# Two attentions and eight experts on one core: four batches' inputs at the head of the queue, the first unit's transposed scores moved ahead, row maxima in one transfer

## The chip, the cores and the metric

The kernel runs on one core of one Trainium2 chip. A core has five engines that run side by side, each with its own instruction stream, in order: PE (matrix multiply, which reads SBUF and writes PSUM), DVE (vector), ACT (scalar functions), POOL (general vector work) and SP (here it only issues transfers). Sixteen DMA engines serve the core; the transfers of this case are put on them mostly by SP, some by ACT and POOL. Engines meet through semaphores: an instruction may wait until a semaphore has reached a value, and raise another one when it is done.

The metric is the device time in microseconds of one execution. The kernel before took 696.34 us, the median of 3 runs (694.67 to 696.98).

## The reference

Eight batches of 256 tokens with 256 features, all in float32. The three stages follow one another:

```
x = layernorm(x + attn(x))      # 16 heads of 16, causal window of 64 keys, Wqkv, bqkv, Wo, bo
x = layernorm(x + xattn(x, ctx))# q = relu(x Wq + bq), k, v = relu(ctx W + b), causal over 256 keys,
                                # softmax(q k / 4) v + q, layer norm with gamma and beta
x = layernorm(x + ffn(x))       # 8 experts, top 2 of a softmax router, capacity 160 per expert
                                # in each of 2 groups of 1024 tokens, relu(x wi) wo, 256 -> 1024 -> 256
```

## The kernel before

**Units.** One attention of one batch is a unit; there are 16, in the order of the list UNITS: self-attention ("s") of batches 0 to 3, then cross-attention ("c") and self-attention in turn. The units 0 to 3 are all self-attention. Everything below is about the first four units, that is the first 100 us.

**What a unit does.** PE projects q and k (QS, KS; line 485; 8 matmuls each, into one of three PSUM banks "work"). ACT adds the bias and rounds to bf16 (line 717), DVE makes two more bf16 parts of what was rounded off (SQ and SK; lines 873, 877, 878), so that three bf16 parts stand for one float32. SP then copies the parts into a tile "arena", six copies for q and six for k, so that a head's six products of parts lie below one another in 96 partitions (line 413). With that, PE makes scores twice:

- The natural scores (jobs N 0 to 11, lines 537 for the mask and 541 for the products, bank "nat"): queries in the partitions. DVE takes the negated maximum of each row (line 926). When all 12 are done, DVE splits the maxima in three bf16 parts (MP, 934 to 937), PE transposes them (MT, 571), ACT copies them to the tile mT (48 rows of 256; line 761), and a transfer writes them as three more rows, partitions 96 to 98, below q's stack (line 425).
- The transposed scores (jobs T 0 to 11, same lines, bank "byk"): keys in the partitions, 99 partitions deep. k's stack has ones in the last three rows, so the maxima are subtracted in the product. ACT takes exp (775) into probs, and after each three jobs PE multiplies with v (PV 0 to 3, line 606), ACT copies the result out (784).

V's projection is VS (line 492), and DVE adds its bias (906). The three rows of ones below each k stack are filled once, for all four stacks, by four transfers at line 364; T 0 of unit 0 waits for them and for the maxima's rows (lines 578 to 580).

**What sets the order.** A function in_order gives every step a slot, a number, and sorts. All engines walk the same list, each doing its part of a step; so the slots set the order on every engine and on SP's queue of transfers. One unit begins every 12 slots (n0). A unit's N jobs stand at n0 to n0 + 11 and its T jobs at n0 + 18 to n0 + 29, so T 0 to T 5 of a unit interleave with N 6 to N 11 of the next, and T 6 to T 11 with N 0 to N 5 of the one after that. QS stands at n0 - 19, KS at n0 - 17.5. LOADS (line 57) gives slots to 13 loads (LD, line 354): V's weights and bias at -10 and -9.9, the rows of ones at -9.8, x of batch 2 at -4, x of batch 3 at 8. SP does them in turn with its other steps, and an SP step that waits holds up all that stand behind it.

Of the kernel before, what the change touches and what calls it, by code (L numbers as in the profile page):

```python
# [6 lines left out]
BF16 = mybir.dt.bfloat16  # L7
# [5 lines left out]
P = 128  # L13
# [11 lines left out]
MR = 3  # L25
# [31 lines left out]
LOADS = (-10, -9.9, -9.8, -4, 8, 15, 15.1, 19, 19.1, 28, 32, 40, 50)  # L57
# [11 lines left out]
def in_order():  # L69
# [6 lines left out]
    for k, (layer, b) in enumerate(UNITS):  # L76
        n0 = first_slot(k)
        if layer == "s":
            for later, earlier in X_BEFORE.items():
                if earlier == b:  # L80
                    add(n0 + 9.6, "LX", UNIT_OF["s", later])
# [77 lines left out]
def attention_and_experts(nc: bass.Bass, a, out):  # L159
    with ExitStack() as ctx:  # L160
# [75 lines left out]
        onesb = sb("onesb", [P, P], BF16)  # L236
# [46 lines left out]
        ident_ready = sem("ident_ready"); masks_ready = sem("masks_ready"); pool_consts = sem("pool_consts"); ones_in = sem("ones_in")  # L283
# [63 lines left out]
        def _(sp):  # L347
# [5 lines left out]

            def LD(i, n, layer, b):

                if i == 0:
                    sp.dma_start(ws[:, :, 2 * D:3 * D], a["w_s_v"]).then_inc(w_s_v_in, 16)
                elif i == 1:
                    sp.dma_start(rows[:, 0:1, :], a["rows"][0:1, :].partition_broadcast(P)).then_inc(bv_in, 16)
                elif i == 2:  # L360
                    sp.wait_ge(pool_cols, 1)
                    ones_rows = arena[KR:KR + MR, :].bitcast(BF16).rearrange("p (i n a b) -> p i n a b", i=PAIRS, n=2, b=P)[:, :, 1, :, :]
                    for pair in range(PAIRS):
                        sp.dma_start(ones_rows[:, pair, :, :], onesb[0:MR, :].unsqueeze(1).broadcast_to([MR, H * T // P, P]))\
                            .then_inc(ones_in, 16)
                elif i == 3:
                    sp.dma_start(x_T(2), a["x_T"][2]).then_inc(x_in[2], 16)
                elif i == 4:
                    sp.dma_start(x_T(3), a["x_T"][3]).then_inc(x_in[3], 16)
                elif i == 5:  # L370
                    sp.dma_start(rows[:, 1:5, :], a["rows"][1:5, :].partition_broadcast(P)).then_inc(rows_in, 16)
                elif i == 6:
                    sp.dma_start(woT[:, :, :], a["w_s_o"]).then_inc(w_s_o_in, 16)
                elif i == 7:
                    sp.dma_start(wc["k"][:, :, :], a["w_c_k"]).then_inc(wc_in["k"], 16)
                elif i == 8:
                    sp.dma_start(cT[:, 0, :, :], a["ctx_T"][0]).then_inc(c_in[0], 16)
                elif i == 9:
                    sp.dma_start(wc["q"][:, :, :], a["w_c_q"]).then_inc(wc_in["q"], 16)
                elif i == 10:  # L380
                    sp.dma_start(cT[:, 1, :, :], a["ctx_T"][1]).then_inc(c_in[1], 16)
                elif i == 11:
# [88 lines left out]
        def _(pe):  # L471
# [103 lines left out]
            def T_(k, j, layer, b):  # L575
                q, ks = stack["q", k % PAIRS], stack["k", k % PAIRS]
                if j == 0:
                    pe.wait_ge(m_rows[k % 2], 16 * MR * (k // 2 + 1))
# [71 lines left out]
            def GP(n, _, layer, b):  # L650
# [3 lines left out]
                def emit(bank):  # L654
                    nc.tensor.matmul(bank[:, 0:NG], tri[:, :], choice[:, n, :], start=True, stop=True)
                    return nc.tensor.matmul(bank[:, NG:2 * NG], onesb[:, :], choice[:, n, :], start=False, stop=True, skip_group_check=True)
# [51 lines left out]
        def _(act):  # L708
# [49 lines left out]
            def MT(k, n, layer, b):  # L758
                bank = computed(act, "MT", k)
                wait(act, m_rows[k % 2], 16 * MR * (k // 2))  # L760
                nc.scalar.activation(mT[:, k % 2, :], bank[0:MR * H, :].bitcast(BF16)[:, 0:T], ACT.Copy).then_inc(released("MT", k), 1)

# [88 lines left out]
        def _(dve):  # L851
# [9 lines left out]
            V.memset(eps[:, :], EPS).then_inc(eps_ready, 1)  # L861
            V.memset(mp[:, :, :, :], 0.0)
# [254 lines left out]
        def _(pool):  # L1117
# [13 lines left out]

            g_.memset(ident[:, :], 0.0)
# [23 lines left out]
            g_.memset(onesb[:, :], 1.0).then_inc(pool_cols, 1)  # L1156
            g_.memset(tri[:, :], 1.0)
# [133 lines left out]
```

## Time and profile before

| | |
|---|---|
| median of 3 runs | 696.34 us |
| the profiled execution | 695.47 us, its span 693.6 us |
| PE busy | 546.2 us, 79% of the span |
| DVE busy | 338.3 us, 49% |
| ACT busy | 218.4 us, 31% |
| POOL busy | 146.7 us, 21% |
| granted TensorE clock, mean | 0.902 |
| DMA queue of SP | 47.69 MB, 41.5% of 16 engines |

The profile page cuts the span in 40 slices of 17.3 us and gives the busy share of each in tenths. PE's row begins 5 2 3 5 9 4 9 8 7 9: of the first six slices, up to 104 us, four are half empty or worse, while later ones mostly stand at 8 or 9. The row of the DMA engines' busy share begins 4 9 5 9 7 5. Both rows are averages; which wait ends last in a stretch is read from the timeline and the list of waits.

### The profile page before, as it was taken

What the parts mean: (1) busy time and instruction counts of PE and PEld (TensorE: products, weight loads), DVE (VectorE), ACT (ScalarE), POOL (GpSimd) and SP (SyncE); (2) the same over time, 40 slices, a digit from 0 to 9 for tenths busy, and PEclk for the clock granted to TensorE, in tenths of its full rate; (3) what the DMA queues carried; (4) which work ended last, traced back from release to release, by engine and by line L of the source; (5) the groups of instructions that cost most, each with busy time, mean ns of one, the idle gap of its engine ahead of it and who ended that gap; (6) DMA issues with size and microseconds to landing.
All of it is one profiled execution on the core that took longest, in us unless ns stands there. A gap on an engine that the chain in (4) does not pass through costs nothing.

```text
span 693.6 us, 12865 instructions
## 1 busy us (share of the span) xinstructions
PE 546.2 (79%) x5092; PEld 422.1 (61%) x5092; DVE 338.3 (49%) x952; ACT 218.4 (31%) x491; POOL 146.7 (21%) x160
## 2 busy tenths in 40 slices
PE   5235949879898998997988678998787977998970
PEld 4122736656675766665766445777576866787860
DVE  4415615667577676776688547633334001222113
ACT  2000424354254453444536233353110100213103
POOL 4000002021021021030241560001111562322320
PEclk9557879999999998999999887899987999999995
DMA  4959756754945944944584553445655212688214
GB/s 97 127 63 140 131 82 110 109 97 75 140 90 88 130 81 85 115 59 69 73 109 63 93 144 79 148 170 176 213 184 168 57 39 59 173 257 288 32 13 131
DMA packets 58503, 78.96 MB, mean 114 GB/s; under 512 B 9630, under 2 KB 51997, under 8 KB 55372
## 3 DMA queue, kind: packets, MB, share of 16 engines
q1 hardware_dynamic: 48844, 47.69, 41.5%
q10 hardware_dynamic: 3456, 25.17, 9.9%
q0 software_dynamic: 6144, 5.29, 4.7%
q8 instruction: 40, 0.66, 0.4%
q14 instruction: 19, 0.16, 0.1%
HBM read 40.32 MB, written 13.74 MB: 78 GB/s over the span
## 4 chain that ended last, share of the span: by engine, by line
PE 32%; DVE 9%; issue 9%; DMA 3%; ACT 3%; SPq 1%; POOL 1%; another core or an unknown queue 0%; ACTq 0%; POOLq 0%; DVEq 0%
PE work L680 10%; PE work L694 8%; PE work L697 2%; PE work L485 2%; PE pv L606 2%; DVE negm L926 1%; PE work L665 1%; PE byk L541 1%; PE work L479 1%; PE byk L537 1%; DVE stats_c L941 1%; DVE r_c L997 1%; DMA arena<-in_ffn_wi 1%; PE work L645 1%; PE nat L541 1%
## 5 line engine op out<-in xcount | busy, mean ns | idle before, releaser
L926 DVE TENSOR_REDUCE negm<-nat 128x4 f32<-128x512 f32 (+2 forms) x192 | 120.4, 641 | 126.5 <-PE nat L541 121.5
L775 ACT ACTIVATE probs<-byk 128x512 f32<-128x512 f32 (+1 forms) x192 | 106.5, 563 | 120.2 <-PE byk L541 118.2
L541 PE MATMUL nat<-arena 96*128 96x128 bf16 (+2 forms) x512 | 74.4, 249 | 0.0
L541 PE MATMUL byk<-arena 99*128 99x128 bf16 (+2 forms) x512 | 73.3, 246 | 0.0
L541 PEld LDWEIGHTS byk<-arena 99*128 99x128 bf16 x512 | 46.6, 101 | 18.9 <-issue 2.7
L541 PEld LDWEIGHTS nat<-arena 96*128 96x128 bf16 x512 | 47.3, 102 | 17.3 <-issue 3.8
L537 PE MATMUL nat<-window_q,identb 128*128 128x384 bf16 (+1 forms) x96 | 36.2, 378 | 19.4 <-DMA arena<-parts_k 13.5
L680 PE MATMUL work<-yn_T,arena 128*128 128x160 f32 x256 | 42.3, 321 | 10.7 <-issue 5.4
L680 PE MATMUL work<-woT,arena 128*128 128x160 f32 x256 | 44.9, 333 | 4.2 <-issue 4.0
L1180 POOL TENSOR_TENSOR resk<-fk,parts_k 128x512 f32<-128x512 f32 x8 | 9.3, 1160 | 172.7 <-ACT fk L717 113.7
L680 PEld LDWEIGHTS work<-yn_T,arena 128*128 128x128 f32 x256 | 38.3, 203 | 12.1 <-issue 5.9
L485 PE MATMUL work<-xT,ws 128*128 128x256 f32 x112 | 30.0, 421 | 18.2 <-DMA xT<-in_x_T 18.2
L680 PEld LDWEIGHTS work<-woT,arena 128*128 128x128 f32 x256 | 40.6, 213 | 5.8 <-issue 5.4
L537 PE MATMUL byk<-window_k,identb 128*128 128x384 bf16 (+1 forms) x96 | 34.4, 358 | 10.5 <-DMA arena<-mT 9.9
L1088 DVE TENSOR_SCALAR target<-v_s,spare 128x1 uint32<-128x1 f32 x10 | 2.1, 213 | 82.2 <-PE work L697 70.2
L717 ACT ACTIVATE parts_q<-work,bias 128x256 bf16<-128x256 f32 x32 | 13.4, 471 | 81.1 <-PE work L485 81.1
L485 PEld LDWEIGHTS work<-xT,ws 128*128 128x128 f32 x112 | 22.8, 212 | 21.8 <-DMA xT<-in_x_T 13.9
L1220 POOL DMA_INDIRECT expert_x<-xres,put x32 | 32.1, 1003 | 12.5 <-issue 10.8
L537 PE MATMUL nat<-causal_q,identb 128*128 128x256 bf16 (+1 forms) x96 | 30.7, 320 | 4.5 <-DVE negm L926 4.2
L537 PE MATMUL byk<-causal_k,identb 128*128 128x256 bf16 (+1 forms) x96 | 31.1, 324 | 2.2 <-DMA arena<-mT 1.2
L1189 POOL TENSOR_TENSOR xres<-xres,rows 128x512 f32<-128x512 f32 x8 | 10.2, 1271 | 106.2 <-DMA rows<-in_rows 63.2
L694 PE MATMUL work<-arena,ws 128*128 128x256 f32 x128 | 30.1, 389 | 0.7 <-ACT ws L829 0.7
(189 smaller groups left out, 959.5 us busy)
## 6 DMA issues: line engine op xcount, KB each, us to landing
arena<-parts_q SPq DMA_DIRECT2D x96, 128.0 KB, 4.8
arena<-parts_k SPq DMA_DIRECT2D x96, 128.0 KB, 5.3
arena<-in_ffn_wi ACTq DMA_DIRECT2D x12, 1024.0 KB, 5.0
arena<-in_ffn_wo ACTq DMA_DIRECT2D x12, 1024.0 KB, 8.3
expert_x<-fq SPq DMA_DIRECT2D x13, 200.0 KB, 5.1
v_s<-expert_x SPq DMA_DIRECT2D x20, 130.0 KB
xres<-in_x SPq DMA_DIRECT2D x8, 256.0 KB, 7.3
cT<-in_ctx_T SPq DMA_DIRECT2D x8, 256.0 KB, 5.4
```

Source lines behind the costliest of these rows:

```text
L485: last = nc.tensor.matmul(bank[:, m * T:(m + 1) * T], w[:, c, m0 + m * P:m0 + (m + 1) * P], tokens[:, c, :], start=(c == 0), stop=(c == C ...
L537: nc.tensor.matmul(bank[:, 0:heads * w].rearrange("p (h t) -> p h t", t=w)[:, :, at:at + mw], identb[:, :], mask[:, :, :].broadcast_to([P, ...
L541: last = nc.tensor.matmul(bank[:, i * w:(i + 1) * w], lhsT, rhs, start=False, stop=(i == heads - 1), skip_group_check=True)
L606: last = nc.tensor.matmul(pv[32 * j:32 * j + 32, o + cols[0]:o + cols[1]], vone[layer][:, b % 2, kt, 4 * g + j, :], probs[:, g % 2, j, src ...
L680: mm = nc.tensor.matmul(bank[:, i * CAP:(i + 1) * CAP], wi[e % WSLOTS][:, c, f * P:(f + 1) * P], xeT[x % 2][:, c, :], start=(c == 0), stop ...
L694: nc.tensor.matmul(bank[:, 0:D], hT[x % 2][:, f, 0:P], wo[e % WSLOTS][:, f, :], start=(f == 0), stop=(f == FC - 1))
L697: mm = nc.tensor.matmul(bank[32 * j:32 * j + REST, D:D + ZW], hT[x % 2][:, f, P:CAP], wo[e % WSLOTS][:, f, j * ZW:(j + 1) * ZW], start=(f ...
L717: last = nc.scalar.activation(dst[:, m, :], bank[:, m * T:(m + 1) * T], func, bias=bias[:, first + m:first + m + 1])
L775: nc.scalar.activation(dst, src, ACT.Exp, scale=0.25).then_inc(exp_ready, 1)
L926: V.tensor_reduce(dst, src, AX, ALU.max, negate=True).then_inc(nat_free[job % 2], 1)
L1189: g_.tensor_tensor(x_b, x_b, bo.unsqueeze(1).broadcast_to([P, QT, D]), ALU.add).then_inc(xb_ready, 1)
L1220: pool.indirect_dma_start(out=x_dram, out_offset=bass.IndirectOffsetOnAxis(ap=put[:, col:col + 1], axis=0), in_=xres[:, tile, :], in_offse ...
```

## The change

Four things change.

1. **Loads.** x of batches 2 and 3, V's weights, V's bias and the rows of ones go out at the head of SP's stream, before any step of the list. The ones are now copied from a tile four times as wide (128 x 512, set by POOL's first instruction), in 8 pieces of 1024 bytes a row instead of 32 of 256. DVE sets v's ones before the first projection.
2. **Unit 2's projections** (QS, KS) move from slots 5 and 6.5 to -1 and -0.9, before unit 0's first scores.
3. **Unit 0's second half.** MP, MT, the V projections of units 0 and 1 (slots 11.4 and 11.41), all 12 T jobs and all 4 PV of unit 0 get slots between 11.2 and 12, that is after unit 0's N 11 and before unit 1's N 0.
4. **Maxima's rows.** One transfer writes 48 rows into three partitions, where three transfers wrote 16 rows into one partition each. For units 0 and 1 ACT issues it, right behind its own copy to mT; for the others SP does.

```
-LOADS = (-10, -9.9, -9.8, -4, 8, 15, 15.1, 19, 19.1, 28, 32, 40, 50)
+LOADS = (13, 15, 19, 19.1, 28, 32, 40, 50)
...
-            for at, name in ((-19, "QS"), (-18, "SQ"), (-17.5, "KS"), (-16.5, "SK"), (8.5, "VS"), (20, "XB"),
+            project = (-25, -24.9) if k == 2 else (-19, -17.5)
+            for at, name in ((project[0], "QS"), (-18, "SQ"), (project[1], "KS"), (-16.5, "SK"), (20, "XB"),
...
+            add(11.4 + k / 100 if k < 2 else n0 + 8.5, "VS", k)
...
-            add(n0 + 18 + j, "T", k, j)
-        add(n0 + 12, "MP", k)
-        add(n0 + 14, "MT", k)
+            add(11.5 + 0.03 * j if k == 0 else n0 + 18 + j, "T", k, j)
+        add(11.2 if k == 0 else n0 + 12, "MP", k)
+        add(11.3 if k == 0 else n0 + 14, "MT", k)
         for g in range(G):
-            add(n0 + 22.2 + 3 * g, "PV", k, g)
+            add(11.5 + 0.03 * (3 * g + 4.2) if k == 0 else n0 + 22.2 + 3 * g, "PV", k, g)
...
-        onesb = sb("onesb", [P, P], BF16)
+        onesb = sb("onesb", [P, 4 * P], BF16)
...
+            sp.dma_start(x_T(2), a["x_T"][2]).then_inc(x_in[2], 16)
+            sp.dma_start(ws[:, :, 2 * D:3 * D], a["w_s_v"]).then_inc(w_s_v_in, 16)
+            sp.dma_start(rows[:, 0:1, :], a["rows"][0:1, :].partition_broadcast(P)).then_inc(bv_in, 16)
+            sp.dma_start(x_T(3), a["x_T"][3]).then_inc(x_in[3], 16)
+            sp.wait_ge(ones_ready, 1)
+            for pair in range(PAIRS):
+                sp.dma_start(stack["k", pair][KR:KR + MR, :, :].rearrange("p h t -> p (h t)").rearrange("p (a b) -> p a b", b=4 * P),
+                             onesb[0:MR, :].unsqueeze(1).broadcast_to([MR, H * T // (4 * P), 4 * P])).then_inc(ones_in, 16)
...
             def MT(k, n, layer, b):          # on SP
-                emptied(sp, "MT", k)
-                for i in range(MR):
-                    sp.dma_start(stack["q", k % PAIRS][KR + i:KR + i + 1, :, :], mT[i * H:(i + 1) * H, k % 2, :])\
-                        .then_inc(m_rows[k % 2], 16)
+                if k >= 2:
+                    emptied(sp, "MT", k)
+                    sp.dma_start(stack["q", k % PAIRS][KR:KR + MR, :, :], mT[:, k % 2, :]).then_inc(m_rows[k % 2], 16)
...
             def MT(k, n, layer, b):          # on ACT
...
+                if k < 2:
+                    emptied(act, "MT", k)
+                    nc.scalar.dma_start(stack["q", k][KR:KR + MR, :, :], mT[:, k, :]).then_inc(m_rows[k], 16)
...
             V.memset(eps[:, :], EPS).then_inc(eps_ready, 1)
+            link(V.memset(vone["s"][:, :, :, :, :], 1.0))
             V.memset(mp[:, :, :, :], 0.0)
...
-                if i in (0, 3):
-                    link(V.memset(vone["s" if i == 0 else "c"][:, :, :, :, :], 1.0))
+                if i == 0:
+                    link(V.memset(vone["c"][:, :, :, :, :], 1.0))
```

The order on PE, before, from the last natural score of unit 0 (the first row is its mask, with nat1 and 384 wide) to the first transposed score of unit 0 (byk0). Work is a PSUM bank, mp the maxima's parts, xT and cT hold x of one batch.

```order
L537 MATMUL nat1<-window_q1,identb 128x384 [waits nat_free1]
L541 MATMUL nat1<-arena 128x192 x2
L537 MATMUL nat0<-window_q,identb 128x512 [waits nat_free0,stacked_k1,stacked_q1]
...
L571 MATMUL work1<-identb,mp 128x128 [waits work_free1,mp_ready]
L571 MATMUL work1<-identb,mp 128x128
...
L485 MATMUL work2<-cT,ws 128x256 [waits work_free2,x_in3]
L485 MATMUL work2<-cT,ws 128x256 x3
L537 MATMUL byk0<-window_k0,identb 128x384 [waits ones_in,m_rows0]
L541 MATMUL byk0<-arena 128x192 x2
L537 MATMUL nat0<-window_q,identb 128x512 [waits nat_free0]
```

The same place in the changed kernel, up to the first natural score of unit 1 (nat0 that waits for stacked_k1).

```order
L533 MATMUL nat1<-window_q1,identb 128x384 [waits nat_free1]
L537 MATMUL nat1<-arena 128x192 x2
L567 MATMUL work0<-identb,mp 128x128 [waits work_free0,mp_ready]
...
L488 MATMUL work1<-ws,xT 128x256 [waits work_free1,w_s_v_in]
L488 MATMUL work1<-ws,xT 128x256 x3
L488 MATMUL work2<-ws,xT 128x256 [waits work_free2]
L488 MATMUL work2<-ws,xT 128x256 x3
L533 MATMUL byk0<-window_k0,identb 128x384 [waits ones_in,m_rows0]
L537 MATMUL byk0<-arena 128x192 x2
...
L533 MATMUL nat0<-window_q,identb 128x512 [waits nat_free0,stacked_k1,stacked_q1]
```

Before, six natural scores of unit 1 and the projection of batch 3's q stood between the maxima of unit 0 and its first transposed score; now two projections of v do, and unit 1's first score comes behind all twelve transposed ones.

SP's stream, before, from the copies of unit 0 to those of unit 2 (arena<-parts_q and arena<-parts_k are the six copies of a stack):

```order
L413 DMA arena<-parts_k 16x8x512 x5
L357 DMA ws<-in_w_s_v 128x2x256
L359 DMA rows<-in_rows 128x256
L364 DMA arena<-onesb 3x32x128 [waits pool_cols]
L364 DMA arena<-onesb 3x32x128 x3
L413 DMA arena<-parts_q 16x8x512 [waits split_q]
L413 DMA arena<-parts_q 16x8x512 x5
L413 DMA arena<-parts_k 16x8x512 [waits split_k]
L413 DMA arena<-parts_k 16x8x512 x5
L367 DMA xT<-in_x_T 128x512
L413 DMA arena<-parts_q 16x8x512 [waits split_q]
```

In the changed kernel the stream begins with all loads, and the stacks of units 0, 1 and 2 follow without anything between them:

```order
L354 DMA xT<-in_x_T 128x512
L356 DMA xT<-in_x_T 128x512
L357 DMA ws<-in_w_s_v 128x2x256
L358 DMA rows<-in_rows 128x256
L359 DMA cT<-in_x_T 128x512
L362 DMA arena<-onesb 3x8x512 [waits ones_ready]
L362 DMA arena<-onesb 3x8x512 x3
L410 DMA arena<-parts_q 16x8x512 [waits split_q]
...
L410 DMA arena<-parts_k 16x8x512 x5
L386 DMA xres<-in_x 128x2x256
```

V's weights, the ones and batch 2's x were queued behind stacks of 12 copies; they now stand ahead of the first stack.

## Rows read from the trace of the kernel before

**Rows 1.** The waits of PE over the whole span: us in total, times, longest.
```profile
PE work L485 <- DMA xT<-in_x_T: 18.2, 2, 13.5
PE nat L537 <- DMA arena<-parts_k: 13.5, 1, 13.5
PE byk L537 <- DMA arena<-mT: 11.2, 3, 8.7
```

**Rows 2.** Timeline of PE, to 113 us: start, length, instructions, idle before, releaser.
```profile
4.75 8.94 PE L485 MATMUL work<-xT,ws 128*128 128x256 f32 x32 [4.75 <-DMA xT<-in_x_T]
...
27.15 0.59 PE L537 MATMUL nat<-window_q,identb 128*128 128x512 bf16 x1 [13.46 <-DMA arena<-parts_k]
...
45.78 3.74 PE L485 MATMUL work<-xT,ws 128*128 128x256 f32 x8 [13.48 <-DMA xT<-in_x_T]
...
68.74 3.78 PE L485 MATMUL work<-cT,ws 128*128 128x256 f32 x8 [5.95 <-DMA cT<-in_x_T]
72.32 0.53 PE L537 MATMUL byk<-window_k,identb 128*128 128x384 bf16 x1
...
96.47 0.50 PE L537 MATMUL byk<-window_k,identb 128*128 128x384 bf16 x1 [8.68 <-DMA arena<-mT]
...
112.12 0.38 PE L537 MATMUL nat<-window_q,identb 128*128 128x512 bf16 x1
```

**Rows 3.** Timeline of SP's issuing.
```profile
11.57 3.90 SPq L413 DMA_DIRECT2D arena<-parts_q  x6
...
20.74 5.26 SPq L364 DMA_DIRECT2D arena<-onesb  x4
...
34.85 0.60 SPq L367 DMA_DIRECT2D xT<-in_x_T  x1
...
87.09 1.82 SPq L425 DMA_DIRECT2D arena<-mT  x3
```

**Rows 4.** Stretches: busy us of PE, PEld, DVE, ACT, POOL, granted clock, DMA share, GB/s.
```profile
20.00:25.00 5.00, 0.00 (x0) 0.00 (x0) 1.76 (x1) 0.00 (x0) 0.00 (x0) 0.50 1.17 117
...
27.50:27.70 0.20, 0.20 (x3) 0.17 (x2) 0.00 (x0) 0.00 (x0) 0.00 (x0) 0.50 0.24 55
...
43.00:44.00 1.00, 0.00 (x0) 0.00 (x0) 0.00 (x0) 0.00 (x0) 0.00 (x0) 0.50 0.21 40
```

**Rows 5.** Timeline of DVE, 20 to 59 us.
```profile
20.11 1.76 DVE L889 MEMSET v_c<- 128x2048 f32 x1 [0.38 <-issue]
...
32.34 0.56 DVE L926 TENSOR_REDUCE negm<-nat 128x2 f32<-128x384 f32 x1 [0.41 <-PE nat L541]
...
50.61 0.87 DVE L873 SCALAR_TENSOR_TENSOR resq<-work,bias,parts_q 128x256 f32<-128x256 f32 x2
...
51.98 0.69 DVE L878 TENSOR_TENSOR parts_q<-resq,parts_q 128x512 bf16<-128x512 f32 x1
...
58.68 0.19 DVE L937 TENSOR_TENSOR mp<-rm,mp 128x32 bf16<-128x32 f32 x1
```

**Rows 6.** The page's group of all maxima: busy us, mean ns, idle before.
```profile
L926 DVE TENSOR_REDUCE negm<-nat 128x4 f32<-128x512 f32 (+2 forms) x192 | 120.4, 641 | 126.5 <-PE nat L541 121.5
```

**Rows 7.** Timeline of PE and ACT, 52 to 85 us.
```profile
52.25 1.92 PE L492 MATMUL work<-ws,xT 128*128 128x256 f32 x8
...
59.26 0.38 ACT L761 ACTIVATE mT<-work 48x256 bf16<-48x256 bf16 x1 [6.57 <-PE work L571]
...
78.52 0.33 PE L537 MATMUL byk<-window_k,identb 128*128 128x384 bf16 x1
...
80.05 0.75 PE L606 MATMUL pv<-probs,v_s 128*32 128x192 f32 x16
...
84.39 0.60 ACT L775 ACTIVATE probs<-byk 128x512 f32<-128x512 f32 x1
```

**Rows 8.** The instructions on tile mT, over the first 460 us: from issue to landing.
```profile
DMA to landing us min/median/max: 1.8/1.9/8.4
```

**Rows 9.** A stretch, columns as in rows 4.
```profile
95.00:100.00 5.00, 3.53 (x16) 2.61 (x17) 1.23 (x2) 0.98 (x2) 1.26 (x1) 0.50 0.04 13
```

More of the change, by code:

```diff
@@ L80, in in_order @@
                 if earlier == b:
-                    add(n0 + 9.6, "LX", UNIT_OF["s", later])
+                    add(n0 + (13 if b < 2 else 9.6), "LX", UNIT_OF["s", later])
             if b == 3:
@@ L282, in attention_and_experts @@
         cleared = sem("cleared"); zeros_ready = sem("zeros_ready")
-        ident_ready = sem("ident_ready"); masks_ready = sem("masks_ready"); pool_consts = sem("pool_consts"); ones_in = sem("ones_in")
+        ident_ready = sem("ident_ready"); masks_ready = sem("masks_ready"); pool_consts = sem("pool_consts"); ones_in = sem("ones_in"); ones_ready = sem("ones_ready")
         v_ones = sem("v_ones"); eps_ready = sem("eps_ready")
@@ L354, in LD @@
             def LD(i, n, layer, b):
                 if i == 0:
-                    sp.dma_start(ws[:, :, 2 * D:3 * D], a["w_s_v"]).then_inc(w_s_v_in, 16)
+                    sp.dma_start(rows[:, 1:5, :], a["rows"][1:5, :].partition_broadcast(P)).then_inc(rows_in, 16)
                 elif i == 1:
-                    sp.dma_start(rows[:, 0:1, :], a["rows"][0:1, :].partition_broadcast(P)).then_inc(bv_in, 16)
+                    sp.dma_start(woT[:, :, :], a["w_s_o"]).then_inc(w_s_o_in, 16)
                 elif i == 2:
-                    sp.wait_ge(pool_cols, 1)
@@ L362, in LD @@
[L362 to L365, printed above, removed]
+                    sp.dma_start(wc["k"][:, :, :], a["w_c_k"]).then_inc(wc_in["k"], 16)
                 elif i == 3:
-                    sp.dma_start(x_T(2), a["x_T"][2]).then_inc(x_in[2], 16)
+                    sp.dma_start(cT[:, 0, :, :], a["ctx_T"][0]).then_inc(c_in[0], 16)
@@ L368, in LD @@
                 elif i == 4:
-                    sp.dma_start(x_T(3), a["x_T"][3]).then_inc(x_in[3], 16)
+                    sp.dma_start(wc["q"][:, :, :], a["w_c_q"]).then_inc(wc_in["q"], 16)
                 elif i == 5:
-                    sp.dma_start(rows[:, 1:5, :], a["rows"][1:5, :].partition_broadcast(P)).then_inc(rows_in, 16)
+                    sp.dma_start(cT[:, 1, :, :], a["ctx_T"][1]).then_inc(c_in[1], 16)
                 elif i == 6:
[L373 to L382, printed above, removed]
@@ L577, in T_ @@
                 if j == 0:
-                    pe.wait_ge(m_rows[k % 2], 16 * MR * (k // 2 + 1))
+                    pe.wait_ge(m_rows[k % 2], 16 * (k // 2 + 1))
                     if k == 0:
@@ L655, in emit @@
                     nc.tensor.matmul(bank[:, 0:NG], tri[:, :], choice[:, n, :], start=True, stop=True)
-                    return nc.tensor.matmul(bank[:, NG:2 * NG], onesb[:, :], choice[:, n, :], start=False, stop=True, skip_group_check=True)
+                    return nc.tensor.matmul(bank[:, NG:2 * NG], onesb[:, 0:P], choice[:, n, :], start=False, stop=True, skip_group_check=True)
                 work_job("GP", n, emit)
@@ L759, in MT @@
                 bank = computed(act, "MT", k)
-                wait(act, m_rows[k % 2], 16 * MR * (k // 2))
+                wait(act, m_rows[k % 2], 16 * (k // 2))
                 nc.scalar.activation(mT[:, k % 2, :], bank[0:MR * H, :].bitcast(BF16)[:, 0:T], ACT.Copy).then_inc(released("MT", k), 1)
+                if k < 2:
+                    emptied(act, "MT", k)
+                    nc.scalar.dma_start(stack["q", k][KR:KR + MR, :, :], mT[:, k, :]).then_inc(m_rows[k], 16)
             def T_(k, j, layer, b):
@@ L1130, in keep @@
                                         pattern=[[0, 1], [step, m.shape[2]]], channel_multiplier=cm)
+            g_.memset(onesb[:, :], 1.0).then_inc(ones_ready, 1)
             g_.memset(ident[:, :], 0.0)
@@ L1155, in _ @@
             link(g_.iota(spare[:, 1:2], [[0, 1]], base=4 * (TOKENS + P), channel_multiplier=1, allow_small_or_imprecise_dtypes=True))
-            g_.memset(onesb[:, :], 1.0).then_inc(pool_cols, 1)
-            g_.memset(tri[:, :], 1.0)
+            g_.memset(tri[:, :], 1.0).then_inc(pool_cols, 1)
             g_.memset(goes_on[:, :], 1.0)
```

## The prediction

> **What bounds the kernel now.** I read the page's 40 slices first: PE is busy 79% of the span, but the half-empty slices lie in the first 104 us. Then PE's waits over the span [rows 1]. Three groups of waits on transfers make 42.9 us (18.2 + 13.5 + 11.2), all but 2.5 us of it before 97 us. The timeline gives the places, and a fourth wait [rows 2]. PE stands still 13.46 us until unit 0's stacks have landed (27.15); 13.48 us until batch 2's x has (45.78); 5.95 us for batch 3's x (68.74), behind which unit 0's first transposed score starts at 72.32; and 8.68 us for the maxima's rows of unit 1 (96.47). From there on PE is nearly always busy. So the kernel is a start of 96 us bound by transfers, and a body bound by PE; the change touches the start.
>
> Why these come late stands in SP's stream [rows 3]. A load that is issued behind a stack lands when the stack's twelve copies have. The copies go at 117 GB/s [rows 4], and 12 of 128 KB make 1.57 MB, so 13.4 us a unit. Batch 2's x, 256 KB, was issued at 34.85 and used at 45.78. Behind the stacks there is also a tail with a DMA share of 0.21 in 43 to 44 us, and 0.24 at 27.5 [rows 4]: three of 16 engines, 0.19, work alone.
>
> The point where both kernels have done the same is the first transposed score of unit 1, T 0 (96.47 before). In both orders unit 0's N and T jobs, unit 1's N and six N of unit 2 are ahead of it; the changed kernel has also done unit 0's last PV. Behind it PE's order is otherwise the same. So I work out when that instruction can start.
>
> **The change part by part.**
>
> Loads first. They add 0.25 + 0.25 + 0.125 + 0.25 MB and 0.1 MB of ones. SP needs four issues of about 0.6 us from 3.9 us on and four for the ones; before, these took 5.26 us [rows 3] in a full queue. In an empty one I take 0.7 each: done by 9.5 us, before the first stack's issue at 11.57 [rows 3]. Cost 0. If the cover fails, each us comes through to 27.15, at most 1.5 us. Unit 0's stacks still end about 27.1: gain 0 there. The stacks of units 1 and 2 follow without a break and end at 27.1 + 13.4 = 40.5 and 53.9, which is no longer awaited by anyone. The waits of 13.48 and 5.95 us lose their cause.
>
> Unit 2's projections early. PE does them behind unit 1's (ended at 13.69 [rows 2]), at 13.7 to 17.6 us, when it idled. On DVE their splits still come behind seven maxima of unit 0.
>
> Unit 0's natural scores. Six took from 27.15 to 32.90 [rows 2, 5], 0.96 each, at the clock of 0.50. Twelve with two splits between on DVE (50.61 to 52.67, so 2.06 each [rows 5]): seven end at 33.9, split, one, split, four more at 0.75 (the scores are ready by then): 33.9 + 2.1 + 0.6 + 2.1 + 3.0 = 41.7. MP ends 0.9 later, 42.6.
>
> Maxima of unit 0. From MP's end (58.87) to the copy's end (59.64) are 0.77 us [rows 5, 7]: 43.4. ACT's issue 0.6 and a landing of 1.9, the median [rows 8]: 45.9. PE meanwhile makes two projections of v, one at half clock (3.74, as at 45.78 [rows 2]) and one at full (1.92 [rows 7]): 43.0 to 48.7. So the transfer is hidden, unless it takes over 4.7 us; SP's six q copies of unit 2 are then on the same engines. The worst landing is 8.4 us [rows 8], for one issued by SP behind a queue at 87.09 [rows 3]: bounds 0 and +3.7 us. I take 0: it is no longer behind that queue.
>
> Here a rule of the Trainium skill bears (DMA: Bandwidth & Descriptors, "Queues, rings and completion order"): each DMA engine serves its rings in turn, and SP and ACT own different rings. By it the ACT transfer waits for one packet of SP's, not for the queue. No run here shows it.
>
> The one transfer instead of three. It saves two issues of 0.61 us (1.82 for three [rows 3]). Against it stands what the tails show: with three destination rows a transfer moves on about three engines [rows 4]. A copy at 117 GB/s over 16 engines takes 70 ns for 512 bytes; 16 of them on one engine are 1.1 us. So the two cancel, 0 us for each of the 16 units; the bounds are -1.2 and +1.1, and it matters only where T 0 waits for it. I carry -0.5 us for the whole body, since the one wait there besides (2.5 us in two, [rows 1, 2]) was on an SP queue with three issues.
>
> The skill says the same of the engines (the same page, "Why a DMA increments its semaphore by 16 and not by 1"): the count is the largest number up to 16 that divides both outer sizes, here 3 and 48, so 3, where 16 and 16 gave 16. The trace's 0.21 and 0.24 agree.
>
> T and PV of unit 0, alone. On PE a T job is 0.66 us at full clock (0.33 mask, 0.33 products [rows 7]). ACT's exp is 0.60 for the form of 512 [rows 7], a bit less for 384, so 0.55, and with two banks and some 0.3 of signalling a job costs (0.66 + 0.55 + 0.3) / 2 = 0.75. Twelve make 9.0, four PV at 0.75 [rows 7] 3.0, and the last exp ahead of the last PV 0.8: 12.8. So 48.7 + 12.8 = 61.5. This is the price of the order: for these 12.8 us DVE has nothing to do, since unit 1's scores stand behind.
>
> Unit 1's natural scores, from 61.5. DVE is the slower side: 12 maxima at 0.64 [rows 6] 7.7, two splits 4.1, the memset of v_c that now falls here 1.76 [rows 5], MP 0.9; 14.5. Ahead of it 0.7 for the first score, and about 2.6 in which DVE waits for PE's two projections and ACT's rounding. MP ends at 79.3, the copy at 80.1, the issue at 80.7; landing 1.9 and 1.1 for three engines: 83.7. Four more N jobs of unit 2 fill that. T 0 of unit 1 at about 84.
>
> Sum: 96.47 - 84.0 = 12.5 us. Unit 0's last PV no longer stands behind: 0.75. The clock: before, PE came out of 8.68 us of idleness and stood at 0.50 through 95 to 100 us [rows 9]; a mask of 384 columns took 0.50 to 0.53 against 0.33 [rows 2, 7]. Four jobs at 0.4 more and a projection at 0.7 more make 2.3 us that go if PE comes in at full clock. It has two idle stretches of 1.5 to 2 us in the N block (the memset, the second split); I count half, 1.1. With the body's 0.5 this is 14.9, so 15 us. What is late next: unit 3's k stack. Its split ends at about 75.6, SP issues it behind q's and two loads, and 1.57 MB and 0.5 MB of loads from 74 on land at about 90; unit 3's first N comes 15.65 us behind T 0 of unit 1 before (112.12 [rows 2]), so about 97: covered.
>
> The profiled execution took 695.47, 1.87 over its span and 0.87 under the median of 696.34. 695.47 - 15 = 680.5; against the median 681.3. I say 681.
>
> **The rivals.**
>
> A, T without partner: the serial block and the DVE-bound block each run slower than I sum, at half clock. For it: the clock stayed at 0.50 through the six scores at 27 to 33, and the DVE-bound block has such gaps. T jobs at 1.06 and N jobs at 1.0 on PE add 12 x 0.3 and 18 x 0.35, and the 2.3 us of clock are not won: T 0 of unit 1 at 92 to 94, gain 3 to 5, and 692. Against: T and PV keep PE busy 12 us in 12.8. Half of it, 4 us given back, is 685.
>
> B, slower: the one transfer on three engines lands late in every unit. From a landing of 1.9 plus what slack a unit has (MT stands four slots ahead of T 0, about 4 us) it decides from 6 us on. At the 8.4 us that rows 8 have as their worst, 2.4 us for each of 14 units are 34, less the 15 won: 715. For it: the tails of 1 to 2 us on three engines [rows 4]. Against: 16 pieces of 512 bytes are a sixth of what made that tail (4 x 32 pieces an engine).
>
> C, nothing comes of it: the start was only early, and the body waits for something else, such as unit 3's stacks or the experts' weights. Then 696. Against: behind 97 us PE's transfer waits are 2.5 us for attention [rows 1, 2].
>
> D, better: the loads' tail gone and the clock full throughout give T 0 at 81 and all 2.3: 696.3 - 15.5 - 0.75 - 2.3 - 0.5 = 677.
>
> **How the numbers follow.** Chances: forecast 0.60 (677 to 685), D and beyond 0.12, A 0.20 (685 to 693), C 0.04, B 0.04. Range 674 to 689: below lies the start's DVE work halved in cover (2 to 3 us more than D), above half of A. A change of 0.3%, 2 us, is what can be told from none. Faster 0.93, within 0.3% 0.03, slower 0.04.
>
> **What would show it.** PE's first scores still at 27 us; no wait for xT or cT ahead of 100 us; unit 0's first transposed score at 47 to 50 and its last PV at 61; unit 1's first score there and none before; T 0 of unit 1 at 84; the landing of maxima's rows of 2 to 4 us. It is wrong if PE waits for maxima's rows over 3 us in any unit, or if the distance from T 0 of unit 1 to the end (597.1 us before) is not 2 to 3 us shorter but longer.

## The result, and the profile after

The changed kernel took 691.85 us (median of the compared runs) against 696.41 of the kernel before on the same chip: 0.994 of it, 95% interval 0.9917 to 0.9964. Faster by 4.6 us, where 15 were forecast; 691.85 is above the range of 674 to 689. The profiled execution took 692.16, its span 689.1 (before 695.47 and 693.6), so the profile shows 4.5 of it.

PE's waits over the span, as in [rows 1] (lines lie four lower in this kernel: L533 is L537 of before, L481 is L485, L488 is L492):

```profile
PE nat L533 <- DVE negm L926: 16.5, 22, 2.1
PE byk L533 <- DMA arena<-mT: 11.9, 3, 6.4
...
PE nat L533 <- DMA arena<-parts_k: 9.7, 1, 9.7
```

The 18.2 us for xT and the 5.95 for cT are gone, but for the 4.8 us of the first load at the start. The wait for the maxima's rows is not: 11.9 us where [rows 1] have 11.2, now in two halves. The timeline says where (PE, answering to [rows 2] and [rows 7]):

```profile
27.35 0.58 PE L533 MATMUL nat<-window_q,identb 128*128 128x512 bf16 x1 [9.70 <-DMA arena<-parts_k]
...
42.20 6.00 PE L488 MATMUL work<-ws,xT 128*128 128x256 f32 x16
54.60 0.50 PE L533 MATMUL byk<-window_k,identb 128*128 128x384 bf16 x1 [6.40 <-DMA arena<-mT]
...
66.24 0.75 PE L602 MATMUL pv<-probs,v_s 128*32 128x192 f32 x16 [0.69 <-ACT probs L774]
66.92 0.39 PE L533 MATMUL nat<-window_q,identb 128*128 128x512 bf16 x1
...
94.68 0.50 PE L533 MATMUL byk<-window_k,identb 128*128 128x384 bf16 x1 [5.13 <-DMA arena<-mT]
```

The last row is T 0 of unit 1, the point up to which both kernels have done the same. It comes at 94.68 where [rows 2] have 96.47: 1.8 us won of the 12.5 forecast. The other 2.7 are in the body behind it (594.4 us, 597.1 before). ACT's rows on the transfer, with what DVE does meanwhile and after:

```profile
42.45 0.38 ACT L757 ACTIVATE mT<-work 48x256 bf16<-48x256 bf16 x1 [14.36 <-PE work L567]
42.85 1.60 ACTq L760 DMA_DIRECT2D arena<-mT  x1
...
67.58 1.16 DVE L926 TENSOR_REDUCE negm<-nat 128x4 f32<-128x512 f32 x2 [18.65 <-PE nat L537]
69.11 1.76 DVE L889 MEMSET v_c<- 128x2048 f32 x1 [0.38 <-PE nat L537]
...
86.51 0.74 ACTq L760 DMA_DIRECT2D arena<-mT  x1
```

Issued at 42.85, used at 54.60: 11.75 us for 24 KB. The second time 8.2 (86.51 to 94.68). And DVE stood idle 18.65 us while PE waited for the transfer and then did unit 0's T and PV jobs alone.

That queue was full before, too. In the kernel before, over its first 100 us, the transfers on mT have these landings:

```profile
DMA to landing us min/median/max: 8.0/8.0/8.4
```

All of them are unit 0's (issued at 62.08 to 63.4); no landing is on record for those of 87.09, used at 96.47. PE had no wait for unit 0's rows then, since it stood for batch 3's x until 68.74. The 1.9 us in [rows 8] is the landing of later units: behind 100 us none took over 3.8.

What the queues did in those 11.75 us is in the rows of DMA packets (queue: packets, MB, share of 16 engines; q1 carries what SP issued, q10 what ACT did). From the span's start to 51.4 us:

```profile
q1 hardware_dynamic: 6907, 6.74, 99.3%
```

In that stretch q10 has no packet. In 51 to 52 us, and in 52 to 53:

```profile
q1 hardware_dynamic: 127, 0.11, 110.8%
q10 hardware_dynamic: 14, 0.01, 5.4%
...
q1 hardware_dynamic: 103, 0.10, 91.5%
q10 hardware_dynamic: 37, 0.02, 21.5%
```

The first packet leaves 8.9 us after the issue (none up to 51.7); then all 51 go in 1.3 us: 48 rows, and 3 more. Up to the issue SP had issued 35 stack copies (name, count, KB each, median us to landing), beside its loads and fills:

```profile
arena<-parts_q SPq DMA_DIRECT2D x18, 128.0 KB, 6.8
arena<-parts_k SPq DMA_DIRECT2D x17, 128.0 KB, 9.3
```

35 x 0.131 MB are 4.59; seven loads of 256 KB 1.84; rows, ones and bias 0.23: 6.66 MB. At 51.4 SP's queue had moved 6.74, at 51.7 6.77. ACT's issue lasts 1.60 us, and in that time SP issued one more copy, which makes 6.79. So the transfer's first packet left when about all that SP had issued before it had left, and ahead of the 1.31 MB of loads that SP issued after it, from 43.72 on. The second transfer is the same: up to 86.51 SP had issued 9.80 MB, and when the first packet left, at 91.7, its queue had moved 9.80.

### The profile page after: what moved, and what is told of

It reads as the page before. It is cut to its first block, busy times and chain, and to the rows that moved or that the text cites. A ratio compares the mean times of both kernels' runs of the same rounds, so it can differ in the third digit from the quotient of the medians.

```text
span 689.1 us, 12832 instructions
## 1 busy us (share of the span) xinstructions
PE 555.4 (81%) x5092; PEld 425.0 (62%) x5092; DVE 338.9 (49%) x952; ACT 218.8 (32%) x491; POOL 146.9 (21%) x160
## 4 chain that ended last, share of the span: by engine, by line
PE 32%; issue 9%; DVE 9%; DMA 3%; ACT 2%; POOL 1%; SPq 1%; ACTq 0%; POOLq 0%; DVEq 0%
PE work L676 10%; PE work L690 8%; PE work L693 3%; PE work L481 2%; PE pv L602 2%; DVE negm L926 1%; PE work L661 1%; PE byk L537 1%; PE byk L533 1%; DMA arena<-in_ffn_wi 1%; DVE stats_c L941 1%; DVE r_c L997 1%; PE nat L537 1%; PE work L641 1%; PE work L475 1%
## 5 line engine op out<-in xcount | busy, mean ns | idle before, releaser
L537 PE MATMUL nat<-arena 96*128 96x128 bf16 (+2 forms) x512 | 76.9, 255 | 0.0
L537 PE MATMUL byk<-arena 99*128 99x128 bf16 (+2 forms) x512 | 74.4, 249 | 0.0
L537 PEld LDWEIGHTS nat<-arena 96*128 96x128 bf16 x512 | 48.5, 105 | 18.0 <-issue 5.3
L537 PEld LDWEIGHTS byk<-arena 99*128 99x128 bf16 x512 | 47.3, 103 | 19.3 <-issue 3.9
L533 PE MATMUL nat<-window_q,identb 128*128 128x384 bf16 (+1 forms) x96 | 38.1, 396 | 22.8 <-DVE negm L926 12.3
L676 PE MATMUL work<-yn_T,arena 128*128 128x160 f32 x256 | 43.8, 329 | 10.1 <-issue 5.1
L676 PEld LDWEIGHTS work<-yn_T,arena 128*128 128x128 f32 x256 | 39.7, 209 | 12.2 <-issue 6.4
L533 PE MATMUL byk<-window_k,identb 128*128 128x384 bf16 (+1 forms) x96 | 35.7, 371 | 12.8 <-DMA arena<-mT 11.5
L533 PE MATMUL byk<-causal_k,identb 128*128 128x256 bf16 (+1 forms) x96 | 31.0, 323 | 4.8 <-issue 4.0
L533 PE MATMUL nat<-causal_q,identb 128*128 128x256 bf16 (+1 forms) x96 | 30.6, 319 | 5.0 <-DVE negm L926 4.2
L1220 POOL DMA_INDIRECT expert_x<-xres,put x32 | 31.9, 996 | 12.5 <-issue 10.8
L481 PE MATMUL work<-xT,ws 128*128 128x256 f32 x112 | 28.2, 406 | 4.8 <-DMA xT<-in_x_T 4.8
L481 PE MATMUL work<-x_T,wq_c 128*128 128x256 f32 x64 | 20.8, 480 | 11.4 <-ACT x_T L751 11.4
L690 PE MATMUL work<-arena,xT 128*128 128x256 f32 x128 | 29.8, 387 | 0.0
```

What stands on the lines that cost most here:

```text
L481: last = nc.tensor.matmul(bank[:, m * T:(m + 1) * T], w[:, c, m0 + m * P:m0 + (m + 1) * P], tokens[:, c, :], start=(c == 0), stop=(c == C ...
L533: nc.tensor.matmul(bank[:, 0:heads * w].rearrange("p (h t) -> p h t", t=w)[:, :, at:at + mw], identb[:, :], mask[:, :, :].broadcast_to([P, ...
L537: last = nc.tensor.matmul(bank[:, i * w:(i + 1) * w], lhsT, rhs, start=False, stop=(i == heads - 1), skip_group_check=True)
L676: mm = nc.tensor.matmul(bank[:, i * CAP:(i + 1) * CAP], wi[e % WSLOTS][:, c, f * P:(f + 1) * P], xeT[x % 2][:, c, :], start=(c == 0), stop ...
L690: nc.tensor.matmul(bank[:, 0:D], hT[x % 2][:, f, 0:P], wo[e % WSLOTS][:, f, :], start=(f == 0), stop=(f == FC - 1))
L1220: pool.indirect_dma_start(out=x_dram, out_offset=bass.IndirectOffsetOnAxis(ap=put[:, col:col + 1], axis=0), in_=xres[:, tile, :], in_offse ...
```

## The experiments

Ratios are against the kernel before in runs on the same chip, with 95% interval. "T 0 of unit 0" and "of unit 1" are PE's first transposed scores, in before at 72.32 and 96.47. The kernels below were timed in three groups of four, each group on one chip together with the kernel before. The theories are: the queue (the transfer is served behind what SP had issued); three engines (the one transfer is slow in itself); a queue of ACT's own (it gets past SP's); and the order itself (A of the rivals). "Stack" is short for the six copies of one side of a unit, "rows" for the maxima's rows.

**Three transfers on sixteen engines.** The changed kernel with ACT issuing a transfer for each row of maxima:

```
+ for i in range(MR):
+     nc.scalar.dma_start(stack["q", k][KR + i:KR + i + 1, :, :], mT[i * H:(i + 1) * H, k, :])
- nc.scalar.dma_start(stack["q", k][KR:KR + MR, :, :], mT[:, k, :])
```

(the counts that PE and ACT wait for are raised to match)

> The changed kernel, but for units 0 and 1 ACT issues three transfers of 16 rows each (as before the change) instead of one of 48 rows. Theory 1 (the transfer is taken up only when the copies that SP issued before it have been served, whichever engine issued it): nothing changes, PE waits for unit 0's maxima's rows about 6.4 us again, then first transposed score at 54 to 55 us, and the time stays within 1 us of 691.9. Theory 2 (the one transfer is slow because only three engines carry it, 16 pieces each, in turn with SP's pieces): with 16 engines and one piece each it lands 2 to 4 us after its issue, the first transposed score starts at 48.2 us, the second wait of 5.1 us falls to 1 to 2, and the time goes to about 682 to 684.

Measured 0.9995 (0.9951 to 1.0039). PE's rows of the two T 0, and then ACT's packets in 49 to 51 us:

```profile
53.89 0.50 PE L533 MATMUL byk<-window_k,identb 128*128 128x384 bf16 x1 [5.54 <-DMA arena<-mT]
...
94.11 0.50 PE L533 MATMUL byk<-window_k,identb 128*128 128x384 bf16 x1 [7.09 <-DMA arena<-mT]
```

```profile
q10 hardware_dynamic: 35, 0.01, 6.0%
```

Issued at 42.79, the first of the three still waits 6.9 us for its first packet (49.7), when SP's queue has moved 6.61 MB. T 0 comes 0.7 us earlier (53.89 against 54.60), but that is no price of the three engines: in this profile SP's queue was 0.08 MB ahead at 42.85 (5.81 moved against 5.73), which is 0.7 us at 117 GB/s. For unit 1 three transfers took longer from first issue to use (83.97 to 94.11, 10.1 us) than the one (8.2). So the wait is not the engines' in the main, and no run here shows what they cost.

**SP's queue held back, once.** The changed kernel; SP issues unit 2's q and k copies only when unit 0's maxima's rows have landed:

```
+ if k in (2,) and side == "q":
+     sp.wait_ge(m_rows[k - 2], 16)
```

> The changed kernel, but SP holds back the twelve copies of unit 2's stacks until unit 0's maxima's rows have landed; the transfer itself is the same, one of 48 rows, issued by ACT. Theory 1 (served in the order of issue over both queues): nothing is ahead of it, it lands within 3 us of its issue at 42.9, the first transposed score starts at about 48.2 us (behind v's projections), 6.4 us earlier, and the time is about 685.5; the copies land at about 60 us, which nobody waits for. Theory 2 (three engines in turn with SP's pieces): also early here, since SP's pieces are gone, so this run tells only together with e1_three_act. Rival 3 (PE waits for something else that ends at 54.6, such as the ones or k's stack): the wait stays and the time is 692.

Measured 0.986 (0.9797 to 0.9922), 683.76. ACT's issue, SP's held copies, the next T 0 on PE:

```profile
42.40 1.36 ACTq L762 DMA_DIRECT2D arena<-mT  x1
...
45.32 3.78 SPq L412 DMA_DIRECT2D arena<-parts_q  x6
...
85.54 0.50 PE L535 MATMUL byk<-window_k,identb 128*128 128x384 bf16 x1 [6.09 <-DMA arena<-mT]
```

The same transfer on the same three engines lands in at most 2.9 us (42.40 to 45.32, where SP's wait for it ends) instead of 11.75. Its first packet leaves at 43.9, so ACT's issue itself is not what is slow. Its packets in 44 to 45 us:

```profile
q10 hardware_dynamic: 44, 0.02, 7.5%
```

T 0 of unit 0 starts at 47.05 with no wait. For unit 1 nothing is held, and PE still waits: 6.09.

**The loads alone.** The changed kernel with unit 0's and 1's VS, MP, MT, T and PV at the slots they had before; the loads first, unit 2's early projections and the one transfer stay:

```
- add(11.5 + 0.03 * j if k == 0 else n0 + 18 + j, "T", k, j)
- add(11.2 if k == 0 else n0 + 12, "MP", k)
- add(11.3 if k == 0 else n0 + 14, "MT", k)
+ add(n0 + 18 + j, "T", k, j)
+ add(n0 + 12, "MP", k)
+ add(n0 + 14, "MT", k)
```

(and VS and PV likewise)

> The changed kernel with the slots of MP, MT, V's projections, T and PV of units 0 and 1 as before the change: the loads stand first, unit 2's projections are early, the maxima's rows go in one transfer, by ACT for units 0 and 1. Theory 1: the order of the T jobs brings nothing by itself; the 19.4 us of waits for batches 2 and 3's x go in both, and the maxima of unit 0 come at about 42 to 43 us in both, behind the same backlog of copies; but here PE has unit 1's scores to do while it waits. Then DVE is used in that time and T 0 of unit 1 comes at 85 to 90 us, and the time is 683 to 688, faster than the changed kernel. Rival (the early T jobs carry the gain): without them it is 694 to 697, the time of the kernel before.

Measured 0.9776 (0.971 to 0.9842), 676.81.

```profile
52.00 0.39 PE L533 MATMUL byk<-window_k,identb 128*128 128x384 bf16 x1 [2.19 <-DMA arena<-mT]
...
75.74 0.50 PE L533 MATMUL byk<-window_k,identb 128*128 128x384 bf16 x1 [7.04 <-DMA arena<-mT]
```

T 0 of unit 1 at 75.74, 20.7 us before where it was, and 18.9 before where the change puts it. The expectation had the direction, but missed by 10 us and more (85 to 90). The loads are worth more than the whole change was forecast to bring; the new order takes most of it back.

**The one transfer alone.** The kernel before with one transfer issued by SP in place of three, in all 16 units:

```
- for i in range(MR):
-     sp.dma_start(stack["q", k % PAIRS][KR + i:KR + i + 1, :, :], mT[i * H:(i + 1) * H, k % 2, :])
+ sp.dma_start(stack["q", k % PAIRS][KR:KR + MR, :, :], mT[:, k % 2, :])
```

(the counts that PE and ACT wait for are lowered to match)

> The kernel before with one change only: SP writes the maxima's rows in one transfer instead of three, in all 16 units. My prediction held this to cost nothing to within 1.2 us a unit where T 0 waits, -0.5 us in all. Theory of the two cancelling: 695.5 to 697, within 0.3% of the kernel before. Rival (three engines make it late in each unit): 14 units at 0.5 to 1 us give 700 or more. Rival (fewer issues help): 694 or less.

Measured 0.9999 (0.9964 to 1.0035). No difference that can be told from none, which here is 2.4 us either way: rival B with its 34 us falls, and if the issues saved bring anything, it is within that.

**SP issues it.** The changed kernel with the transfer of units 0 and 1 back on SP:

```
- if k >= 2:
+ if k >= 0:
      ...
      sp.dma_start(stack["q", k % PAIRS][KR:KR + MR, :, :], mT[:, k % 2, :])
```

(and ACT's own issue taken out)

> The changed kernel, but SP issues the one transfer of maxima's rows for units 0 and 1 as well, at their place in its stream, which is behind the copies of unit 2's k stack. Theory 1 (what counts is what was issued ahead, not whose queue it is): issued at about 43.8 instead of 42.9 us, behind at most one or two more copies, it lands at 54 to 55.5 us, the first transposed score starts there, and the time is within 2 us of the changed kernel. Rival (ACT's own queue did help, by being served in turn): it lands with the end of the queue, loads included, at 57 us or later, and the kernel is 3 us or more slower.

Measured 1.0009 (0.9977 to 1.0041). SP's issue and PE's T 0:

```profile
44.77 0.77 SPq L422 DMA_DIRECT2D arena<-mT  x1
...
55.97 0.50 PE L533 MATMUL byk<-window_k,identb 128*128 128x384 bf16 x1 [7.92 <-DMA arena<-mT]
```

11.2 us from issue to use, where ACT's took 11.75; T 0 is 0.5 us later than expected. T 0 comes 1.4 us later, and SP comes to the issue 1.9 us later. A queue of its own got the transfer past nothing that SP had issued. What ACT's issue does bring is an earlier place in that order, as unit 1 shows more clearly: SP comes to it only at 89.56, behind all of unit 3's k copies and two loads (ACT at 86.51), and T 0 of unit 1 is at 98.87, 4.2 us behind the changed kernel and 2.4 behind the kernel before. (That the whole kernel is not slower than before is within the interval.)

**Held back twice.** The changed kernel; unit 2's q and k copies wait for unit 0's rows, unit 3's k copies for unit 1's:

```
+ if (k, side) in ((2, "q"), (3, "k")):
+     sp.wait_ge(m_rows[k - 2], 16)
```

> The changed kernel with unit 2's twelve copies held until unit 0's maxima's rows have landed (as in e3_quiet_one) and the six copies of unit 3's k stack held until unit 1's have. Theory 1: at the second transfer's issue (76.4 us) only the end of unit 3's q copies and two loads are ahead; it lands at about 82, and the first transposed score of unit 1 starts there instead of at 85.5. The time is 680 to 681, 3 us below e3_quiet_one, and 11 below the changed kernel. Rival: unit 3's k stack now comes late and PE waits for it at about 95 us: no gain against e3_quiet_one.

Measured 0.9757 (0.9697 to 0.9818), 672.45 against 689.72.

```profile
42.80 1.35 ACTq L762 DMA_DIRECT2D arena<-mT  x1
...
45.70 3.79 SPq L412 DMA_DIRECT2D arena<-parts_q  x6
...
81.19 0.50 PE L535 MATMUL byk<-window_k,identb 128*128 128x384 bf16 x1 [0.86 <-DMA arena<-mT]
```

T 0 of unit 1 at 81.19: the forecast's 84 is reached, and passed, once the transfers land about as the sum assumed. Two waits on SP give back 13.5 us at that point, and the kernel is faster than expected (680 to 681), even by its ratio alone.

**Loads alone, held back.** The old slots as above, unit 2's k copies (q's are needed too soon there) and unit 3's k copies held:

```
+ if (k, side) in ((2, "k"), (3, "k")):
+     sp.wait_ge(m_rows[k - 2], 16)
```

> The slots of before for MP, MT, V, T and PV (as in e2_loads_only), the loads first, and SP holds the six copies of unit 2's k stack until unit 0's maxima's rows have landed, those of unit 3's k stack until unit 1's have. Theory 1: the wait of 2.19 us at 52.0 goes (the projection of batch 3's q ends at 49.8), and that of 7.04 at 75.7 falls to 0 to 1, since at the issue at 66 us two or three copies fewer are ahead and q's are done at 65. T 0 of unit 1 at 66 to 68 us, the span 662 to 664, 1.2% faster than e2_loads_only and about 3.5% than the kernel before. Rival: unit 2's or 3's k stack is now late, PE waits 3 us or more for it at its first natural score, and nothing is won over e2_loads_only.

Measured 0.9573 (0.9515 to 0.9632), 659.61.

```profile
68.61 0.34 PE L535 MATMUL byk<-window_k,identb 128*128 128x384 bf16 x1 [3.37 <-DMA arena<-mT]
```

That is faster than expected (1.2% below the loads alone; it is 2.1% by the ratios), but the wait of 3.37 us is not the 0 to 1 that was expected. 68.61 against 81.19 is about the order's own price with most of the queue out of the way: 12.6 us, with waits for rows of 3.37 and 0.86 in it. (The two do not hold quite the same copies.) Most of it can be unit 0's T and PV jobs done alone, which with the queue held take 10.4 us (47.86 to the end of this row):

```profile
57.50 0.75 PE L604 MATMUL pv<-probs,v_s 128*32 128x192 f32 x16 [0.69 <-ACT probs L776]
```

The rest is not taken apart here. A part of it may be the granted clock: in 70 to 90 us it is 0.66 in that kernel, where PE does unit 1's natural scores alone and waits for DVE between them, and 0.94 in this one.

**The same, the memset moved.** DVE sets v_c's ones with unit 1's SK instead of inside its natural scores:

```
  def SK(...):
      ...
+     if k == 1:
+         link(V.memset(vone["c"][:, :, :, :, :], 1.0))
```

> b1_loads_hold, and DVE sets v_c's ones (1.76 us) behind the splits of unit 1, at 18 us, where it idles, instead of among unit 1's maxima. In the changed kernel PE waited 2.1 us for DVE at that memset. Expected: PE's wait of 1.5 us at 45.8 goes, up to 1.5 us faster than b1_loads_hold; or 0, if PE waits for unit 0's maxima's rows there anyway.

Measured 0.9586 (0.9523 to 0.9649), 659.58. PE's wait of 1.5 us at 46 us goes, T 0 of unit 1 comes 0.8 us earlier (67.82), and the time can't be told from the one above.

**The changed kernel again,** beside the last three:

> The changed kernel itself, on the same chip as the kernels below, since the kernel before has differed by up to 1% between chips and the effect is 0.6%. Expected from the first timing: 0.992 to 0.996 of the kernel before. If it is 1.000, the gain of the change is nothing that can be told from none.

Measured 0.9916 (0.9878 to 0.9955), 685.34 against 690.34: T 0 at 54.55 and 94.49, waits of 6.27 and 5.98. The first result repeats in another set of runs.

**Unit 2's early projections.** The loads alone, those projections at their old slots too:

```
- project = (-25, -24.9) if k == 2 else (-19, -17.5)
+ project = (-19, -17.5)
```

> e2_loads_only (the loads first, the T jobs at their old slots) with unit 2's projections at their old slots too. Theory: the loads alone bring the gain, and the early projections only fill PE while it waits; they then take 3.8 us of PE among unit 0's scores, of which DVE's splits hide half, since PE also waits for maxima's rows at 50 us: T 0 of unit 1 at 75 to 78 us (75.74 in e2_loads_only), 0.975 to 0.982 of the kernel before. Rival: without early projections unit 2's copies go out later, the maxima's rows find an empty queue, and it is faster than e2_loads_only.

Measured 0.9669 (0.961 to 0.9729), 669.04.

```profile
53.62 0.34 PE L533 MATMUL byk<-window_k,identb 128*128 128x384 bf16 x1 [0.60 <-DMA arena<-mT]
...
76.03 0.50 PE L533 MATMUL byk<-window_k,identb 128*128 128x384 bf16 x1 [6.87 <-DMA arena<-mT]
```

T 0 of unit 1 at 76.03 against 75.74: the early projections bring nothing by themselves. The ratio is below what was expected (0.975 to 0.982), and below the 0.9776 with them. The two are from different sets of runs and their intervals overlap, so a difference is not shown; the traces give no reason for one ahead of T 0.

**The best again.** Loads alone, held back, beside the changed kernel:

> The same kernel as b1_loads_hold, on the chip of the changed kernel. Expected 0.957 of the kernel before, as there, and 3.5% below the changed kernel; T 0 of unit 1 at 68.6 us.

Measured 0.9557 (0.9503 to 0.9611), 658.66; T 0 of unit 1 at 67.89, with a wait of 2.15. Its waits of PE:

```profile
PE nat L535 <- DVE negm L928: 11.9, 19, 1.8
...
PE nat L535 <- DMA arena<-parts_k: 9.6, 1, 9.6
```

On one chip: 690.34 before, 685.34 changed, 658.66 this one, 3.9% under the changed kernel. It is the fastest found.

**Both of unit 3's stacks held.** As the one with the moved memset, but unit 3's q copies wait as well:

```
- if (k, side) in ((2, "k"), (3, "k")):
+ if (k, side) in ((2, "k"), (3, "q")):
```

> b2_loads_hold_mem, but SP holds both of unit 3's stacks until unit 1's maxima's rows have landed, not k's alone. PE's wait of 3.5 us for them at 67.8 goes, since only loads are ahead of them at 61. Unit 3's twelve copies then go out at 64 and land at 78 to 80; its first natural score, 12.5 us behind T 0 of unit 1, is due at 77. Expected a new wait of 0 to 3 us there, and in all 0 to 3.5 us faster than b2_loads_hold_mem. Rival: the new wait takes all of it back.

Measured 0.9615 (0.9564 to 0.9665), 663.07.

```profile
74.31 3.75 PE L483 MATMUL work<-cT,wk_c 128*128 128x256 f32 x8 [8.82 <-issue]
```

PE's wait for unit 1's rows is gone, and T 0 comes at 63.88, 4.0 us earlier than in the best. But a wait of 8.82 us appears ahead of the k projection of layer c, where 0 to 3 were expected and for another thing. The profile gives no releaser for it, but SP's issues explain it. The two loads of that projection stand in SP's stream behind the held copies, are issued at 67.53 and 68.18 (58.23 and 58.88 in the best) and land in 5.4 and 6.0 us, the second one so at 74.2, just ahead of the projection. The rival of the expectation holds: holding a queue costs whatever else stands in it.

## Why the prediction was wrong

**The step that failed** is "Maxima of unit 0", where the sum takes 0 for the transfer: "I take 0: it is no longer behind that queue." It was behind it. The mechanism of the +3.7 bound was seen, its row (8.4 us in [rows 8]) was at hand, and it was set aside for the reason that ACT has a queue of its own. The row was misread as well: the 8.4 us are not those of the issue at 87.09 but of unit 0's own, at 62 to 63, and none of the landings on record for the first 100 us was under 8.0. The 1.9 us that the sum takes, for unit 1 too, belong to later units. From issue to use it was 11.75 us here, more than the bound even. In bytes the queue was not longer than at 87.09 of the kernel before (0.93 MB issued and not moved, against 1.04), but all of it was stack copies, which go at 117 GB/s and make 7.9 us; at 87.09 half of it was loads, and where loads go the rate can be over 300 (324 GB/s in 68 to 70 us). In numbers, T 0 of unit 1 by the sum's own steps:

| step | forecast | measured |
|---|---|---|
| first natural scores | 27.1 | 27.35 |
| maxima in mT | 43.4 | 42.83 |
| two projections of v end | 48.7 | 48.20 |
| T 0 of unit 0 | 48.7 | 54.60 |
| T and PV of unit 0 | 12.8 | 12.4 |
| natural scores of unit 1, to MP's end | 17.8 | 18.6 |
| MP's end to T 0 of unit 1 | 4.7 | 9.1 |
| T 0 of unit 1 | 84.0 | 94.68 |

5.9 - 0.4 + 0.8 + 4.4 are the 10.7 us that went. 10.3 of them are the two landings. Held back, the same transfers give 81.19: shown, not only argued.

**The rule of the Trainium skill** (DMA: Bandwidth & Descriptors, "Queues, rings and completion order"), that each DMA engine serves its rings in turn, supported the failed step, and no row then spoke of it. Here the measurement decides against the use I made of it: with SP's queue full, no q10 packet in 8.8 us; with it empty, the whole transfer in 2.9 at most. Whether the rings are served in turn below some common stage can't be seen; issues on SP and on ACT took effect in the order of their issue.

**Loads first** was right: both waits went, the scores still begin at 27, and the fills in the empty queue delayed them by 0.2 us at most (27.35 for 27.15). What I did not do is price this part without the rest. It alone puts T 0 of unit 1 at 75.74.

**The order's price** was named ("This is the price of the order: for these 12.8 us DVE has nothing to do"). Its size of 12.8 was met (12.4), in part by chance: the sum takes full clock, but PE came out of 6.40 us of idleness and stood at 0.50 through 54.6 to 60 us; at full clock, with the queue held, the same jobs take 10.4. It was set only against the waits, never against the old order with the loads first. There PE does natural and transposed scores of two units in turns, so ACT's exp and DVE's maxima run beside each other. The runs with and without the order differ by 18.9 us at T 0 of unit 1, and by 12.6 with the queue held.

**The one transfer** was right so far as can be told: 0 (0.9999, within 2.4 us). Its term of 1.1 us for three engines where T 0 waits is not shown by any run: the 0.7 us of the first experiment is as much as SP's queue was ahead in its profile. In the argument against B, 16 pieces an engine are an eighth of 4 x 32, and a quarter of their bytes, not a sixth; nothing hangs on it.

**The body** was forecast 2.35 us shorter and is 2.7 shorter, but the agreement is not more than chance. The 1.1 us in it for the clock rest on PE coming in at full clock, and it came out of a wait of 5.13 us with masks of 0.50 and 0.53 again. And the size is not shown: from T 0 of unit 1 to the end the profiles of these kernels, whose work there is the same, have between 587 and 599 us, the changed kernel itself 594.4 and 590.2.

**Rivals.** A gave 692 and T 0 of unit 1 at 92 to 94, near the result, but by another mechanism: the half clock did come in part (0.50 for the first half of the T jobs, 0.69 on the mean in 70 to 90 us), but its slow blocks did not (T and PV took 12.4, the N block 18.6), so its agreement is chance. B and C fall (0.9999; T 0 of unit 1 moves the end). D's 81 for T 0 came true only with the queue held. "It is wrong if PE waits for maxima's rows over 3 us in any unit" was the sign to watch: 6.40 and 5.13.

## What to carry to other kernels

In these runs a small urgent transfer lands behind the bulk that was issued before it, whichever engine issues it; make it early by issuing the bulk later, and see what else stands behind the held copies. When a landing time is taken for a sum, take it from the stretch that the sum is about: here the median of the first 460 us was 1.9 us, and that of the first 100 was 8.0. When a change has several parts, work out the sum for each part without the others: here one was worth 20.7 us and another cost 18.9. An order that finishes one unit before the next begins leaves one engine idle for as long as that takes; compare it with the order it replaces, not with the wait it is meant to remove.

## What was not expected of the hardware

- Issues on SP and ACT were served in the order of issue, 24 KB taking 11.75 us behind about 1 MB of SP's (0.95 MB in 43 to 51 us), 11.2 us when SP issued it itself. Where the order is kept, on the way to the engines or in them, no run here shows.
- With SP's queue empty, three engines move the 48 rows of 512 bytes in about 0.6 us (43.9 to 44.5). The tail of ones that shows a share of 0.21 in [rows 4] was longer since it had 32 pieces of 256 bytes to a row, in four transfers.
- The kernel before had medians of 696.4, 693.6, 689.7 and 690.3 us in the four sets of comparisons, so only ratios within a set compare. The chip is not all of it: the second and the fourth have the same chip on record. One wait differs within one kernel: PE's for an expert's x (`parts_q<-expert_x`) was 0.4 us in the first profile of the changed kernel and 9.8 in the second, though their times differ the other way. Why stays open.
